# A third pair of weight chunks by seven products, and a search laid out by a table

## The chip, the cores and the metric

The kernel runs on one core of a Trainium2 chip. The metric is the time of one execution on the device, in microseconds (us). Three runs of the kernel before took 2345.66, 2346.05 and 2346.59 us; the median is 2346.05 us.

TensorE (PE in the profile) multiplies. VectorE (DVE), ScalarE (ACT) and GpSimd (POOL) do elementwise work, and SyncE (SP) issues nearly all transfers. Each engine runs its own instructions in order; they wait for each other through semaphores. Results of TensorE land in eight PSUM banks of 128 x 512 float32.

## The reference

Over 2048 tokens of width 1024 it computes a gated layer whose smaller half is set to zero, and a layer with a routed part, and adds both to the input:

```python
xn = (x - mean) / sqrt(var + 1e-5)
s = silu(xn @ w_gate.T)                       # 2752 units
s[the 1376 smallest |s| of each token] = 0
a = (s * (xn @ w_up.T)) @ w_down.T
h = relu(xn @ up_w) ** 2                      # 2048 units
shared = h @ down_w
routed = ((xn @ fc1_w) @ expert_w * (sum of the two largest of xn @ gate_w)) @ fc2_w
out = x + a + layernorm(shared + routed) * gamma + beta
```

## The kernel before

**Precision.** Each float32 operand is split into a high part, as TensorE rounds it, and a low part, the rest. A product is three matmuls: high by high, high by low, low by high (lines L880 to L882). All weights are split once, in block 0, and stored back to memory as pairs; later blocks load the pairs.

**Tiling.** There are four blocks of 512 tokens, that is four token tiles of 128. Weights come in chunks of 512 columns. The six gate chunks are gate 0 to 5 (gate 5, the "tail", has 392 columns here: 192 gate units, 8 routing logits, 192 up units), the five other up chunks up 0 to 4, and so on. One row of 128 weights of one chunk is a **granule**: one slot of a ring, and for the four token tiles 4 x 3 = 12 matmuls. A chunk has 8 granules. Granules have numbers m within a block, and all engines loop over the same m. The class Plan lays down at which m an engine reads which result. "At m" says only where an instruction stands in its engine's row: what it really waits for are semaphores.

**Seven products.** In blocks 1 to 3, gate 0 and 1 form a pair, and gate 2 and 3 another. A pair is a 2 x 2 block matrix product, done by seven block products instead of eight (Strassen's scheme in Winograd's form). Each has 4 granules of two token tiles, so of 6 matmuls. Four of the seven take mixed weights (T1 to T4, sums of weight rows), which VectorE makes in block 0 in `mix` (L1091 to L1096, once per four granules of a pair, two buffers `mixes`), and SyncE stores to `mixed_w` (L542). The results are put together by VectorE adds in `read_fast` (L1113, L1114). In block 0 the pairs are computed the plain way, 16 granules of 12 matmuls each.

**Order in a block.** Block 0: pair 0, pair 1 (32 granules), gate 5, gate 4, latent, hidden 0 and 1, routed 0 and 1, shared 0 and 1, hidden 2 and 3, up 4, shared 2, shared 3, up 0 to 3, out 0, out 1. Blocks 1 to 3 begin with gate 5 and then take both pairs by seven products. In block 0 a granule's weights are loaded raw, ScalarE makes the high part (L717), GpSimd the low part (L679); during the search GpSimd makes both (L675, L679).

**The search.** The threshold of each token is found bit by bit: 31 steps. In a step VectorE counts, in one pass each over 128 x 2816 magnitudes, for token tiles 0 and 1 (L1204), ScalarE for tiles 2 and 3 (L729), and VectorE settles the bit (L1193, L1196). The steps stand three granules apart in every engine's row, and between them stand VectorE's reads of other results. After the last step VectorE counts ties (L1212 to L1222) and masks: `mask` (L1266) multiplies the up values by "magnitude at least the threshold", group by group (a group is what one gate chunk holds), in the order gate 4, 5, 0, 1, 2, 3. GpSimd multiplies in the gate magnitudes (L702), TensorE turns the product chunks (L900, the first turn after granule out0 - 5, where out0 is the first granule of out 0), and out 0 can use them.

**Banks.** A chunk has four banks, one per token tile: set 0 is banks 0 to 3, set 1 banks 4 to 7, and chunks alternate. A chunk can't open before its banks were emptied by whoever reads the chunk before it in the same set. The first turn needs bank 0, which up 2 fills.

Of the kernel before, what the change touches and what calls it, by code (L numbers as in the profile page):

```python
# [60 lines left out]
FAST = 2  # L61
PRODUCTS = ["A11 B11", "S2 T2", "A12 B21", "S1 T1", "S4 B22", "S3 T3", "A22 T4"]
PRODUCT_BANK = [[4, 6, 0, 2, 4, 6, 0], [2, 4, 6, 4, 6, 0, 2]]
# [11 lines left out]
SET = {("gate", c): c % 2 for c in range(2 * FAST)}  # L75
SET.update({name: s % 2 for s, (name, n) in enumerate(_gates + _rest)})

# [4 lines left out]
def _first_pair(p):  # L82

    found = []
    for n in range(4 * HALF):
        c, k = 2 * p + n % 4 // 2, n // 4 + n % 2 * HALF
        found.append(Granule(("pair", p), n, ("gate", c), range(TILES), k == 0, n // 4 == HALF - 1 and n % 2 == 1,
                             (("gate", c), k)))
    return found


def _fast_pair(p):

    found = []
    for q, product in enumerate(PRODUCTS):
        right = product.split()[1]
        for k in range(HALF):
            if right[0] == "T":
                source = ("mixed", p, k, int(right[1]) - 1)
            else:  # L100
                source = (("gate", 2 * p + int(right[2]) - 1), k + HALF * (int(right[1]) - 1))
# [8 lines left out]

class Plan:


    def __init__(self, later):
        self.later = later
        found = []
        if later:
            found += _plain(*_gates[0])
        for p in range(FAST):
            found += _fast_pair(p) if later else _first_pair(p)  # L120
        for step in _gates[later:] + _rest:
            found += _plain(*step)
        self.granules = found
# [9 lines left out]
        self.read_at = {end[key] + LAG: key for key in end if key[0] in ("gate", "latent", "routed", "shared")}  # L133
        if later:
            del self.read_at[end[_gates[0][0]] + LAG]
            self.read_at[end[_gates[0][0]] + FAST_LAG] = _gates[0][0]
        self.read_up_at = {end[("up", g)] + (2 if g in (0, GROUPS[-1]) else LAG): ("up", g) for g in range(GC - 1)}
        self.search_at = {end[_gates[1][0]] + LAG + 1 + 3 * k: k for k in range(BITS)}

        order = [d for c in range(0, 2 * FAST, 2) for d in ((c + 1, c) if later else (c, c + 1))]  # L140
        order = [GC - 1, *order] if later else [*order, GC - 1]
        self.signs_before = {c: i + (i > order.index(GC - 1)) for i, c in enumerate([*order, GC - 2])}
# [1267 lines left out]
```

## Time and profile before

| | |
|---|---|
| median of three runs | 2346.05 us |
| profiled execution, its own time | 2345.21 us |
| its span | 2343.4 us |
| TensorE | 2330.9 us busy, 10576 matmuls |
| VectorE | 1602.3 us |
| ScalarE | 1054.3 us |
| GpSimd | 710.4 us |
| granted TensorE clock | 1.00 |

An engine's busy time is a sum over its instructions; the span is from the first to the last instruction of the core. TensorE is busy nearly without a break, so only two things change the time: how many matmuls there are, and whether TensorE has to wait.

### The profile page before, as it was taken

Reading aid. Unit: us, or ns where it says so; the run is one execution under the profiler, and the core shown is the slowest. Engines: PE = TensorE matmul, PEld = TensorE weight load, DVE = VectorE, ACT = ScalarE, POOL = GpSimd, SP = SyncE. Lnnn points to the kernel's source line nnn. Section 1 sums busy time; section 2 is a strip of 40 time slices with the busy share of each in tenths; the row PEclk is TensorE's granted clock in tenths of the full one; section 3 lists DMA queues with packets and bytes.
Section 4 is the critical chain, followed back from the end, with each engine's and each line's share of the span. In section 5 each row is a group of like instructions: output and inputs, shape, how many; then the busy total and the mean of one; then the engine's idle time right before and its main releaser. Section 6 shows DMA issues by size and latency. Waiting matters only on the chain.

```text
span 2343.4 us, 27578 instructions
## 1 busy us (share of the span) xinstructions
PE 2330.9 (99%) x10576; PEld 1940.5 (83%) x10576; DVE 1602.3 (68%) x1797; ACT 1054.3 (45%) x1199; POOL 710.4 (30%) x598
## 2 busy tenths in 40 slices
PE   8999999999999999999999999999999999999999
PEld 6888888888888888888888888888888888888887
DVE  4349999976255999876235699986723478997650
ACT  3248776133244877602124586740213368773010
POOL 5467878796450101040034010104004301000500
PEclk9999999999999999999999999999999999999999
DMA  7798889879886665655777666665667765556555
GB/s 284 283 391 293 292 271 324 292 241 316 279 294 199 193 195 192 214 191 187 235 247 245 208 193 194 194 210 189 206 218 259 251 192 195 194 193 213 183 189 180
DMA packets 182020, 545.83 MB, mean 233 GB/s; under 512 B 19328, under 2 KB 28544, under 8 KB 181888
## 3 DMA queue, kind: packets, MB, share of 16 engines
q1 hardware_dynamic: 181888, 544.06, 69.2%
q8 instruction: 84, 1.38, 0.2%
q14 instruction: 48, 0.39, 0.1%
HBM read 419.14 MB, written 124.85 MB: 232 GB/s over the span
## 4 chain that ended last, share of the span: by engine, by line
PE 99%; DMA 0%; DVE 0%; POOL 0%; DVEq 0%; ACT 0%; issue 0%
PE bank L880 32%; PE bank L882 32%; PE bank L881 32%; PE bank L900 2%; PE bank L891 1%; PE bank L973 0%; PE bank L974 0%; DMA rows<-x_dram 0%; DVEq L1035 0%; POOL expert L650 0%; DVE stats L1034 0%; POOL fc L654 0%; DVE acc L1275 0%; ACT expert L815 0%; DVE mv L1036 0%
## 5 line engine op out<-in xcount | busy, mean ns | idle before, releaser
L1204 DVE TENSOR_SCALAR_CACHE_REDUCE junk_v<-mag,cand 128x2816 bf16<-128x2816 f32 x248 | 780.3, 3146 | 8.8
L729 ACT ACTIVATE junk_s<-mag,cand 128x2816 uint8<-128x2816 f32 x248 | 655.6, 2644 | 222.6 <-DVE cand L1196 202.1
L880 PE MATMUL bank<-w,tok 128*128 128x512 f32 (+1 forms) x1108 | 426.3, 385 | 0.0
L882 PE MATMUL bank<-w,tok 128*128 128x512 f32 (+1 forms) x1108 | 424.9, 384 | 0.0
L881 PE MATMUL bank<-w,tok 128*128 128x512 f32 (+1 forms) x1108 | 424.8, 383 | 0.0
L679 POOL TENSOR_TENSOR w<-raw,w 128x512 fp32r<-128x512 f32 (+1 forms) x196 | 268.6, 1374 | 77.3 <-ACT w L717 67.6
L880 PE MATMUL bank<-w,prod_t 128*128 128x512 f32 x672 | 269.4, 401 | 0.0
L691 POOL TENSOR_TENSOR squares<-squares 128x512 f32<-128x512 f32 x64 | 69.0, 1078 | 640.4 <-ACT hidden L809 640.3
L882 PE MATMUL bank<-w,prod_t 128*128 128x512 f32 x672 | 262.8, 391 | 0.0
L881 PE MATMUL bank<-w,prod_t 128*128 128x512 f32 x672 | 261.9, 390 | 0.0
L880 PE MATMUL bank<-tok,w 128*128 128x512 f32 x640 | 249.0, 389 | 0.0
L881 PE MATMUL bank<-tok,w 128*128 128x512 f32 x640 | 249.0, 389 | 0.0
L882 PE MATMUL bank<-tok,w 128*128 128x512 f32 x640 | 249.0, 389 | 0.0
L882 PEld LDWEIGHTS bank<-w,tok 128*128 128x128 f32 x1108 | 208.0, 188 | 38.6
L881 PEld LDWEIGHTS bank<-w,tok 128*128 128x128 f32 x1108 | 208.1, 188 | 37.7
L880 PEld LDWEIGHTS bank<-w,tok 128*128 128x128 f32 x1108 | 208.0, 188 | 37.7
L869 ACT ACTIVATE prod_t<-bank 128x512 fp32r<-128x512 f32 x88 | 52.4, 596 | 402.2 <-PE bank L900 402.2
L702 POOL TENSOR_TENSOR prod<-prod,mag 128x512 f32<-128x512 f32 x88 | 122.2, 1411 | 338.4 <-DVE prod L1266 338.0
L880 PE MATMUL bank<-w,hidden 128*128 128x512 f32 x512 | 199.3, 389 | 0.0
L881 PE MATMUL bank<-w,hidden 128*128 128x512 f32 x512 | 199.2, 389 | 0.0
L882 PE MATMUL bank<-w,hidden 128*128 128x512 f32 x512 | 199.2, 389 | 0.0
L882 PEld LDWEIGHTS bank<-w,prod_t 128*128 128x128 f32 x672 | 126.1, 188 | 27.5
(140 smaller groups left out, 3307.4 us busy)
## 6 DMA issues: line engine op xcount, KB each, us to landing
w<-split_w SPq DMA_DIRECT2D x546, 512.0 KB, 4.2
split_w<-w SPq DMA_DIRECT2D x196, 512.0 KB, 4.9
w_more<-split_w SPq DMA_DIRECT2D x42, 512.0 KB, 4.9
w<-mixed_w SPq DMA_DIRECT2D x78, 256.0 KB, 3.2
rows<-x_dram SPq DMA_DIRECT2D x32, 512.0 KB, 5.2
raw<-w_down_dram SPq DMA_DIRECT2D x44, 256.0 KB, 4.0
raw<-w_up_dram SPq DMA_DIRECT2D x40, 256.0 KB, 3.5
w<-split_w SPq DMA_DIRECT2D x24, 392.0 KB, 3.7
```

Source lines behind the costliest of these rows:

```text
L679: pool.tensor_tensor(lo, words, hi, ALU.subtract).then_inc(lo_ready, 1)
L691: pool.tensor_tensor(squares[:, n, :], squares[:, n, :], squares[:, n, :], ALU.mult).then_inc(squared, 1)
L702: pool.tensor_tensor(prod[:, c, :, units], prod[:, c, :, units], mag[:, c, :, units], ALU.mult).then_inc(prod_ready, 1)
L729: act.activation(junk_s[:, :, :], mag[:, :, t, :], ACT.Sign, scale=-1.0, bias=cand[:, t:t + 1], accum_out=cnt[:, t:t + 1]).then_inc(counte ...
L869: act.activation(prod_t[0][:, c, :], banks[bank][:, :], ACT.Copy).then_inc(operand_hi, 1)
L880: pe.matmul(out, left[0], right[0], start=first, stop=False)
L881: pe.matmul(out, left[0], right[1], start=False, stop=False)
L882: return pe.matmul(out, left[1], right[0], start=False, stop=last)
L891: last = pe.transpose(banks[2 * (t % 2) + h][:, k * P:(k + 1) * P], rows_of(t)[:, (h * HK // 2 + k) * P:(h * HK // 2 + k + 1) * P], ident[ ...
L900: last = pe.transpose(banks[bank][:, t * P:(t + 1) * P], prod[:, c, t, :], ident[:, :])
L1204: dve.tensor_scalar(junk_v[:, :, :], mag[:, :, t, :], cand[:, t:t + 1], float(1 - (GATED - KEPT)), ALU.is_lt, ALU.add, accum_out=cnt[:, t: ...
```

## The change

A third pair is formed of gate 4 and up 4 (`PAIRS`). Block 0 computes it the plain way, after pair 1 and ahead of gate 5, and mixes its weights; blocks 1 to 3 take it by seven products, straight after pair 1. Up 4 leaves its place between hidden 3 and shared 2. As its results are sums now, VectorE applies the signs to up 4 in one instruction, `sign_up`.

The search begins after the last gate chunk: in block 0 after gate 5, with the first step at m = 60 instead of 52, and in blocks 1 to 3 after the third pair, with the first step at m = 96 instead of 76. Its layout is now written as tables (`VECTOR_TILES`, `STEP_AT`), which hold what stood there before: two tiles on each engine, three granules apart. Shared 2 and shared 3 are interleaved by half chunks, so that both close within 4 granules, at the end of 16. The squares of hidden 2 and 3 stand one granule apart instead of two; in blocks 1 to 3 their low parts, and those of hidden 0 and 1, are made by GpSimd instead of VectorE. The buffer of latent's high part moves into `acc`, and ScalarE waits for what that needs.

```diff
+PAIRS = [(("gate", 0), ("gate", 1)), (("gate", 2), ("gate", 3)), (("gate", GC - 2), ("up", GC - 2))]
+FAST = len(PAIRS)
-PRODUCT_BANK = [[4, 6, 0, 2, 4, 6, 0], [2, 4, 6, 4, 6, 0, 2]]
+PRODUCT_BANK = [[4, 6, 0, 2, 4, 6, 0], [2, 4, 6, 4, 6, 0, 2], [4, 6, 0, 4, 6, 0, 2]]
-_gates = [(("gate", GC - 1), HK), (("gate", GC - 2), HK)]
+_tail = (("gate", GC - 1), HK)
-          (("hidden", 2), HK), (("hidden", 3), HK), (("up", GC - 2), HK), (("shared", 2), HK), (("shared", 3), HK)]
+          (("hidden", 2), HK), (("hidden", 3), HK), (("shared", 2), HK), (("shared", 3), HK)]
+VECTOR_TILES = [range(2) for k in range(BITS)]
+STEP_AT = [3 * k for k in range(BITS + 1)]
...
+        at = [m for m, g in enumerate(found) if g.step in (("shared", 2), ("shared", 3))]
+        found[at[0]:at[-1] + 1] = [found[m] for m in sorted(at, key=lambda m: (found[m].k // HALF, m))]
...
-        self.search_at = {end[_gates[1][0]] + LAG + 1 + 3 * k: k for k in range(BITS)}
+            last = end["fast", FAST - 1, len(PRODUCTS) - 1]
+            self.fast_at.update({last + 2: (FAST - 1, 5), last + 3: (FAST - 1, 6)})
+            self.signs_at[last + 4] = (FAST - 1, 6)
+            first = last + 5
+        else:
+            first = end[_tail[0]] + LAG + 1
+        self.search_at = {first + STEP_AT[k]: k for k in range(BITS)}
...
-        self.hidden_at = {end[("hidden", i)] + LAG + 1 + 2 * t: (i, t) for i in range(SC) for t in range(TILES)}
+        self.hidden_at = {end[("hidden", i)] + LAG + 1 + (2 if i < 2 else 1) * t: (i, t) for i in range(SC) for t in range(TILES)}
...
+                        if b:
+                            pool.wait_ge(squared, b * SC * TILES + i * TILES + t + 1)
+                            pool.tensor_tensor(hidden[1][:, n, :], squares[:, n, :], hidden[0][:, n, :],
+                                               ALU.subtract).then_inc(hidden_lo, 1)
...
+            def sign_up(b):
+                ks = slice(4 * (GC - 2), 4 * (GC - 1))
+                dve.wait_ge(signs_done, b * (GC + 1) + PLANS[b].signs_before[GC - 2] + 1)
...
+                dve.scalar_tensor_tensor(out=prod[:, ks, :, :], in0=positive[:, ks, :, :], scalar=-1.0,
+                                         in1=prod[:, ks, :, :], op0=ALU.add, op1=ALU.mult).then_inc(up_signed, 1)
```

VectorE's row in block 0, just ahead of the first pass of the search. `positive` and `mag` of 128x2048 are the reading of a whole gate chunk, the small operations onto `prod` the end of reading gate 5, `junk_v` the count. Before:

```order
L1160 SCALAR_TENSOR_TENSOR prod<-positive,bank 128x128
L1160 SCALAR_TENSOR_TENSOR prod<-positive,bank 128x64
L1132 TENSOR_SCALAR positive<-mag 128x2048
L1136 TENSOR_SCALAR mag<-mag 128x2048
L1345 MEMSET cand 128x4
L1204 TENSOR_SCALAR junk_v,cnt<-mag,cand 128x2816 x2
```

And now (line numbers are those of the changed kernel):

```order
L1199 SCALAR_TENSOR_TENSOR prod<-positive,bank 128x128
L1199 SCALAR_TENSOR_TENSOR prod<-positive,bank 128x64
L1389 MEMSET cand 128x4
L1243 TENSOR_SCALAR junk_v,cnt<-mag,cand 128x2816 x2
L1232 TENSOR_SCALAR refused<-cnt 128x4
L1235 SCALAR_TENSOR_TENSOR cand<-cand,refused 128x4
```

The reading of gate 4 is gone from this place; the search starts straight after gate 5 has been read.

VectorE's row in block 0, after the count of ties: masks, and between them the reads of up 1 and up 2 (`prod<-positive,bank`). Before:

```order
L1266 SCALAR_TENSOR_TENSOR prod<-mag,thr,prod 128x4x128 x4
L1266 SCALAR_TENSOR_TENSOR prod<-mag,thr,prod 128x2x128 x4
L1266 SCALAR_TENSOR_TENSOR prod<-mag,thr,prod 128x4x128 x4
L1181 SCALAR_TENSOR_TENSOR prod<-positive,bank 128x4x128 x4
L1266 SCALAR_TENSOR_TENSOR prod<-mag,thr,prod 128x4x128 x4
L1181 SCALAR_TENSOR_TENSOR prod<-positive,bank 128x4x128 x4
L1266 SCALAR_TENSOR_TENSOR prod<-mag,thr,prod 128x4x128 x4
L1378 TENSOR_TENSOR prod_t_54<-bank,prod_t_53 128x512 x3
```

And now:

```order
L1308 SCALAR_TENSOR_TENSOR prod<-mag,thr,prod 128x4x128 x4
L1220 SCALAR_TENSOR_TENSOR prod<-positive,bank 128x4x128 x4
L1308 SCALAR_TENSOR_TENSOR prod<-mag,thr,prod 128x2x128 x4
L1308 SCALAR_TENSOR_TENSOR prod<-mag,thr,prod 128x4x128 x8
L1220 SCALAR_TENSOR_TENSOR prod<-positive,bank 128x4x128 x4
L1308 SCALAR_TENSOR_TENSOR prod<-mag,thr,prod 128x4x128 x4
L1422 TENSOR_TENSOR prod_t_54<-bank,prod_t_53 128x512 x3
```

The read of up 1 moves ahead of the masks of groups 5 and 0. What stands ahead of the read of up 2 is the same set of instructions as before. The read of up 0, which stood right behind the last step of the search, now stands two steps ahead of its end, in all blocks.

## Rows read from the trace of the kernel before

**Rows 1.** The page: the chain that ended last, share of the span by engine

```profile
PE 99%; DMA 0%; DVE 0%; POOL 0%; DVEq 0%; ACT 0%; issue 0%
```

**Rows 2.** Waits of PE: us in total, times, longest

```profile
PE bank L891 <- DVE rows L1050: 8.8, 2, 7.9
```

**Rows 3.** Timeline of PE (start, length, instruction): first matmuls of stretches

```profile
37.74 0.39 PE L880 MATMUL bank<-w,tok 128*128 128x512 f32 x1
124.78 0.34 PE L880 MATMUL bank<-w,tok 128*128 128x392 f32 x1
141.80 0.39 PE L880 MATMUL bank<-w,tok 128*128 128x512 f32 x1
```

**Rows 4.** Windows: the search of block 0, then of block 1

```profile
168.00:428.00 260.00, 260.00 (x1148) 215.06 (x1147) 253.85 (x229) 191.63 (x168) 205.39 (x209) 1.00 0.87 297
741.00:999.00 258.00, 258.00 (x1140) 213.71 (x1139) 235.46 (x229) 192.63 (x168) 17.26 (x16) 1.00 0.62 198
```

**Rows 5.** Timeline of DVE: mixes start; below, landing of the mixes' stores

```profile
82.84 0.69 DVE L1091 TENSOR_TENSOR mixes<-raw 128x512 f32<-128x512 f32 x1 [9.25 <-DMA mixed_w<-mixes]
96.10 1.00 DVE L1091 TENSOR_TENSOR mixes<-raw_more 128x512 f32<-128x512 f32 x1 [3.78 <-DMA mixed_w<-mixes]
120.26 0.92 DVE L1091 TENSOR_TENSOR mixes<-raw_more 128x512 f32<-128x512 f32 x1 [8.75 <-DMA mixed_w<-mixes]
...
DMA to landing us min/median/max: 6.2/6.7/8.1
```

**Rows 6.** Timeline of POOL: low parts of granules 14, 30 and 38

```profile
66.52 1.29 POOL L679 TENSOR_TENSOR w<-raw_more,w 128x512 fp32r<-128x512 f32 x1 [3.69 <-ACT w L717]
...
116.32 1.29 POOL L679 TENSOR_TENSOR w<-raw_more,w 128x512 fp32r<-128x512 f32 x1 [2.59 <-ACT w L717]
...
135.74 1.04 POOL L679 TENSOR_TENSOR w<-raw,w 128x392 fp32r<-128x392 f32 x1 [2.59 <-ACT w L717]
```

**Rows 7.** Timeline, block 0: gate 5 read, first pass of the search

```profile
145.68 0.26 ACT L786 ACTIVATE mag<-bank 128x128 f32<-128x128 f32 x1
...
151.23 1.33 DVE L1160 SCALAR_TENSOR_TENSOR prod<-positive,bank 128x128 f32<-128x128 uint8 x8
...
168.13 3.15 DVE L1204 TENSOR_SCALAR_CACHE_REDUCE junk_v<-mag,cand 128x2816 bf16<-128x2816 f32 x1
```

**Rows 8.** Timeline, block 0: up 4 read, last settling, masks, up 2 read, first turn

```profile
368.07 2.47 DVE L1181 SCALAR_TENSOR_TENSOR prod<-positive,bank 128x512 f32<-128x512 uint8 x4
...
428.00 0.58 DVE L1193 TENSOR_SCALAR refused<-cnt 128x4 int32<-128x4 f32 x1
...
447.62 13.57 DVE L1266 SCALAR_TENSOR_TENSOR prod<-mag,thr,prod 128x512 f32<-128x512 f32 x12 [4.77 <-issue]
...
468.79 2.47 DVE L1181 SCALAR_TENSOR_TENSOR prod<-positive,bank 128x512 f32<-128x512 uint8 x4
...
479.31 0.60 PE L900 MATMUL bank<-ident,prod 128*128 128x128 f32 x4
```

**Rows 9.** Timeline, block 1: two steps, up 0, masks, up 1 and 2, first turn

```profile
978.05 3.15 DVE L1204 TENSOR_SCALAR_CACHE_REDUCE junk_v<-mag,cand 128x2816 bf16<-128x2816 f32 x1
...
984.91 3.15 DVE L1204 TENSOR_SCALAR_CACHE_REDUCE junk_v<-mag,cand 128x2816 bf16<-128x2816 f32 x1
...
996.77 2.73 DVE L1181 SCALAR_TENSOR_TENSOR prod<-positive,bank 128x512 f32<-128x512 uint8 x4 [5.53 <-PE bank L882]
...
1017.13 13.12 DVE L1266 SCALAR_TENSOR_TENSOR prod<-mag,thr,prod 128x512 f32<-128x512 f32 x12 [3.73 <-issue]
...
1032.57 4.90 DVE L1266 SCALAR_TENSOR_TENSOR prod<-mag,thr,prod 128x512 f32<-128x512 f32 x4
...
1042.94 2.73 DVE L1266 SCALAR_TENSOR_TENSOR prod<-mag,thr,prod 128x512 f32<-128x512 f32 x4
...
1053.02 0.60 PE L900 MATMUL bank<-ident,prod 128*128 128x128 f32 x4
```

**Rows 10.** Windows: the first 13 us

```profile
0.00:13.00 13.00, 3.91 (x16) 3.14 (x16) 5.24 (x13) 5.04 (x9) 3.45 (x8) 1.00 0.84 317
```

More of the change, by code:

```diff
@@ L85, in _first_pair @@
     for n in range(4 * HALF):
-        c, k = 2 * p + n % 4 // 2, n // 4 + n % 2 * HALF
-        found.append(Granule(("pair", p), n, ("gate", c), range(TILES), k == 0, n // 4 == HALF - 1 and n % 2 == 1,
-                             (("gate", c), k)))
+        name, k = PAIRS[p][n % 4 // 2], n // 4 + n % 2 * HALF
+        found.append(Granule(("pair", p), n, name, range(TILES), k == 0, n // 4 == HALF - 1 and n % 2 == 1, (name, k)))
     return found
@@ L159, in __init__ @@
         self.tokens_load += [out1 + 7, out1 + 11]
-        if later:
-            self.fast_at = {end[("fast", p, q)] + FAST_LAG: (p, q) for p in range(FAST) for q in range(len(PRODUCTS))}
-            self.signs_at = {end[("fast", p, q)] + FAST_LAG + 3: (p, q) for p in range(FAST) for q in (5, 6)}
 TURN_AFTER = [5, 9, 13, 17]
@@ L254, in highs @@
     return 2 * TILES + b * HIGHS + HIGH_FROM[kind] + n
-NV = TILES // 2
-NS = TILES - NV
-VECTOR_TILES, SCALAR_TILES = range(NV), range(NV, TILES)
+SCALAR_TILES = [range(len(tiles), TILES) for tiles in VECTOR_TILES]
 SQUARE_LAG = 2
@@ L852, in _ @@
                         square_hidden(b, *plan.hidden_at[m])
-                    for n, t in enumerate(SCALAR_TILES):
-                        if m - n in plan.search_at:
-                            count(b, plan.search_at[m - n], n, t)
+                    for n in range(TILES - 1):
+                        k = plan.search_at.get(m - n)
+                        if k is not None and n < len(SCALAR_TILES[k]):
+                            count(b, k, n, SCALAR_TILES[k][n])
                     for t in range(TILES):
@@ L1098, in read_fast @@
             def read_fast(b, p, q):
-                c, d = 2 * p, 2 * p + 1
+                c, d = (name[1] for name in PAIRS[p])
+                right = mag if PAIRS[p][1][0] == "gate" else prod
                 for j in range(2):
@@ L1136, in read_gate @@
                     dve.tensor_scalar(bits, bits, 0x7FFFFFFF, None, ALU.bitwise_and).then_inc(mag_ready, 1)
+            def sign_up(b):
+                ks = slice(4 * (GC - 2), 4 * (GC - 1))
+                dve.wait_ge(signs_done, b * (GC + 1) + PLANS[b].signs_before[GC - 2] + 1)
+                for j in range(2):
+                    for q in (4, 5):
+                        bank, value = emptied(b, ("fast", FAST - 1, q, j))
+                        dve.wait_ge(bank_emptied[bank], value)
+                dve.scalar_tensor_tensor(out=prod[:, ks, :, :], in0=positive[:, ks, :, :], scalar=-1.0,
+                                         in1=prod[:, ks, :, :], op0=ALU.add, op1=ALU.mult).then_inc(up_signed, 1)
             def read_logits(b):
@@ L1261, in mask @@
                 for t in range(TILES):
-                    bank, value = emptied(b, ("up", g, t) if g < GC - 1 else ("gate", g, t))
-                    dve.wait_ge(bank_emptied[bank], value)
+                    if b and g == GC - 2:
+                        dve.wait_ge(up_signed, b)
+                    else:
+                        bank, value = emptied(b, ("up", g, t) if g < GC - 1 else ("gate", g, t))
+                        dve.wait_ge(bank_emptied[bank], value)
                     if g == GC - 1:
```

75 lines of the change are left out of this document (42 added, 33 removed).

## The prediction

> **What bounds the kernel now.** I read the chain that ended last first: TensorE holds 99% of it [rows 1]. The list of TensorE's waits shows why: its largest entry is 8.8 us, at the start; nothing later is worth a row [rows 2]. So the time is the sum of TensorE's instructions, and the timeline gives their pace. In block 0, 32 granules lie between 37.74 and 124.78 [rows 3]: 2.72 us a granule, 226.7 ns a matmul of 512 columns. The 8 granules of gate 5 take 17.02 us, 2.13 each. Less work for TensorE is time won, as long as nobody makes it wait, so next I read how close the others are. The windows show VectorE busy for 253.85 of 260 us in the search of block 0, and 235.5 of 258 in block 1 [rows 4]. GpSimd, which in block 0 splits weights, is busy 205 us in the first and 17 in the second. Two places matter: block 0, where VectorE has nothing to spare, and the first turn, where its work must be done.
>
> **The gain.** Gate 4 and up 4 cost 2 x 8 x 12 = 192 matmuls in a block. By seven products they cost 7 x 4 x 6 = 168. That is 24 fewer, in three blocks 72; 72 x 226.7 ns = 16.3 us. Block 0 has as many as before. If nothing waited, the profiled execution would take 2345.2 - 16.3 = 2328.9 us.
>
> **Block 0, the preparation of weights.** Low parts have to be ready before TensorE takes a granule. That of granule 14 is ready at 66.52 + 1.29 = 67.8 and TensorE takes it at 37.74 + 14 x 2.72 = 75.8, 8.0 us later. For granule 30 the same reckoning gives 117.6 against 119.3, for granule 38 136.8 against 137.5 [rows 3, 6]. So 16 pair granules cost TensorE 43.5 us and the preparation 49.8, and the lead is eaten to 0.8 us. The reason is in the mixes: each waits for the landing of a store [rows 5], SyncE sends the next raw loads only when a mix is made, and three rounds take 120.26 - 82.84 = 37.4 us, 12.5 for four granules. The third pair adds four such rounds, and I see nothing that would speed them up. The low part of granule 54, the former 38, is then due at 136.8 + 49.8 = 186.6, and TensorE could take it at 37.74 + 48 x 2.72 + 6 x 2.13 = 181.1. TensorE waits 5.5 us in all here. It doesn't add to what follows, since VectorE is later still.
>
> **Block 0, the search.** Before, it began at 168.13, 4 us after gate 4. Now it begins after gate 5. ScalarE reads gate 5 at 145.68, after its own splits, and VectorE is done with it at 152.6 [rows 7]. With 49.8 us on top, the first pass starts at 202.5, 34.3 us later than before. TensorE's work ahead of out 0 is the same as before, so the turns should still come at 479.3. From the first pass to the last settling VectorE worked without a break for 259.9 us [rows 7, 8]. The same 31 steps, 16 low parts and reads stand there now, except the read of up 4 (2.4 us), now ahead of the search. The last settling is due at 428.0 + 34.3 - 2.4 = 459.9. Before, the read of up 2 began 40.8 us after the settling [rows 8], and the same instructions lie between, in another order. So bank 0 is free for the first turn at 459.9 + 40.8 + 0.7 = 501.4, against 479.3: 22.1 us late. The nearer stops on the way (up 3 needs the read of up 1, at 482.9 to 485.3 against 468.2; shared 2 needs the low parts of hidden 3) are inside this.
>
> This takes every mask at its slow rate. Twelve masks took 13.57 us beside GpSimd's work, four without it took 2.73 [rows 8, 9]. While TensorE stands still, GpSimd has no slot to fill until the first mask is made; so I give the first four the fast rate, 2.4 us less: 19.7 us late. If all masks had it, it would be 12.7. The ends are 12.7 and 22.1, the value 19.7.
>
> On this term the Trainium skill has a rule: SBUF — State Buffer, Who interferes with whom, says that a VectorE instruction with two SBUF inputs and a GpSimd instruction that reads SBUF exclude each other for a whole instruction. By it the masks would cost their own 0.7 us plus at most one GpSimd instruction each, and the term would lie between the same two ends; the rows agree so far. The count passes, with one such input, would be untouched.
>
> **Blocks 1 to 3.** Here TensorE reaches the end of up 0 a fixed 20 granules before the first turn, in both kernels. In block 1 the read of up 0 ended at 999.5 and the turn came at 1053.0: 53.5 us [rows 9]. Behind that read there stand now two more steps (2 x 6.86 = 13.7), then settling, ties and the pause before the masks (1017.13 - 999.5 = 17.6), masks of four groups with the read of up 1 (1037.5 - 1017.1 = 20.3), and the first tile of up 2, 0.7: 52.3 us. So 1.2 us remain of 15. The read of up 0 itself should be on time: 29 steps (199 us), four reads of 2.7 and about 6 us before the first pass make 216, TensorE takes 88 x 2.72 = 239. VectorE also gets rid of the low parts of the squares; GpSimd, at 17 of 258 us, takes them for nothing. `sign_up` is one instruction for four reads, inside those 6 us. I put this term at 0, with 0 to 2 us a block as its bounds.
>
> **The sum.** 2345.2 - 16.3 + 19.7 = 2348.6 us for an execution like the profiled one, which lay 0.8 under the median: 2349.4. Both terms are large and nearly cancel.
>
> **The rivals.**
> First, block 0 keeps up and the gain comes through. For it: the rounds of mixes are a chain of latencies, not a full memory, so an earlier raw load would shorten them. Against it: VectorE is without idle time afterwards. If preparation kept TensorE's pace (6.3 us less) and gate 5 were read as it closes (145.7 - 141.8 = 3.9 less), the delay would be 9.5: 2339.2 us. With no delay at all it would be 2329.7. I give both 17%.
> Second, the slower one: blocks 1 to 3 each wait at the first turn. The place is bank 0, held by up 2; it decides once VectorE is more than 1.2 us late behind up 0, and each further microsecond counts three times. For it: the squares of hidden 2 and 3 stand closer, so ScalarE's counts can come later, and GpSimd's products slow the masks. Against it: VectorE was idle 22.5 of 258 us in block 1's search, and with the read of up 1 among them the masks meet fewer products. At 3 us late: 3 x 1.8 = 5.4 more, 2354.8 us. 25%.
> Third, TensorE's clock falls in the waits of block 0. In the first 13 us TensorE was busy 3.9 us and the granted clock read 1.00 [rows 10], so the waits so far left it at the upper level, 2.4 GHz. A granule at 1.2 GHz would cost 5.4 instead of 2.7 us; two of them lost make 5.4 us and 2354.8. 3%.
> The Trainium skill (TensorE: Matmul & The Clock Gate, Why this matters for your kernels) warns that idle gaps between matmuls drop the clock to half; by it the waits of block 0 would add some microseconds. The first window doesn't bear it out.
>
> **How the numbers follow.** The forecast, 55%: 2349.4, by its bounds 2342.4 to 2351.8. About 0.2%, 4.7 us, is what a measurement of this kernel can tell from no change: 2341.4 to 2350.7 count as the same. Of the forecast's 55 I put 46 there and 9 above; the first rival gives 17 to faster; of the second and third, 24 to slower and 4 to the same. Faster 0.17, same 0.50, slower 0.33. The range must reach into the second rival and to the edge of the first: 2342 to 2355.
>
> **What would show it.** TensorE has 10576 - 72 = 10504 matmuls. In block 0 its waits appear at low parts of weights around 160 to 187 us (some 5.5 us) and at VectorE's results until the first turn, which comes near 499 instead of 479.3; the first pass starts near 202.5, the last settling near 460. Out 0 and out 1 of block 0 keep their length. A block 1 to 3 is 5.4 us shorter, with its first turn on time. The forecast is wrong if the first pass starts before 195, if VectorE's 257 us between first pass and last settling shrink, or if blocks 1 to 3 show waits before their first turn.

## The result, and the profile after

The changed kernel is slower: 2356.11 us (median of five runs, 2355.81 to 2361.0) against 2346.05 in the same comparison, a ratio of 1.0047 with a 95% interval of 1.0032 to 1.0062. The forecast was 2349.4, its range 2342 to 2355. The profiled execution took 2355.98 us, its span is 2354.2: 10.8 us more than before, where 3.4 more were forecast.

The list of TensorE's waits (us in total, times, longest), where [rows 2] had one entry worth a line:

```profile
PE bank L919 <- DVE rows L1078: 8.7, 2, 7.8
PE bank L928 <- DVE prod L1220: 7.1, 1, 7.1
PE bank L908 <- DVE hidden L1383: 6.6, 2, 3.5
PE bank L908 <- POOL w L697: 3.1, 4, 0.9
PE bank L908 <- ACT mag L809: 1.6, 2, 1.0
```

The first is the start, as before. The others are all in block 0: the first turn waits for the read of up 2 (L1220), shared 2 for low parts of hidden, three granules of the third pair and one of gate 5 for low parts of weights (L697), and the openings of up 4 and gate 5 for banks that ScalarE has yet to read (L809). The chain that ended last, by engine, which was all TensorE in [rows 1], says the same:

```profile
PE 79%; DVE 13%; DMA 4%; issue 1%; SPq 1%; ACT 1%; POOL 1%; DVEq 0%; ACTq 0%
```

The later blocks did what was forecast. TensorE's first matmuls of block 1 and block 2, before and after:

```profile
622.34 0.34 PE L880 MATMUL bank<-w,tok 128*128 128x392 f32 x1
...
1196.03 0.34 PE L880 MATMUL bank<-w,tok 128*128 128x392 f32 x1
```

```profile
649.08 0.34 PE L908 MATMUL bank<-w,tok 128*128 128x392 f32 x1
...
1217.51 0.34 PE L908 MATMUL bank<-w,tok 128*128 128x392 f32 x1
```

A block takes 568.4 us instead of 573.7, 5.3 less, three times. But block 1 begins 26.7 us later. 26.7 - 3 x 5.3 = 10.8, the whole difference. So everything is in block 0, whose stops answer to [rows 7, 8] (VectorE, then TensorE's first turn and the matmuls behind it):

```profile
202.97 3.15 DVE L1243 TENSOR_SCALAR_CACHE_REDUCE junk_v<-mag,cand 128x2816 bf16<-128x2816 f32 x1
...
461.98 0.17 DVE L1232 TENSOR_SCALAR refused<-cnt 128x4 int32<-128x4 f32 x1
...
481.80 3.18 DVE L1308 SCALAR_TENSOR_TENSOR prod<-mag,thr,prod 128x512 f32<-128x512 f32 x4 [4.12 <-issue]
...
484.89 2.47 DVE L1220 SCALAR_TENSOR_TENSOR prod<-positive,bank 128x512 f32<-128x512 uint8 x4
487.29 16.01 DVE L1308 SCALAR_TENSOR_TENSOR prod<-mag,thr,prod 128x256 f32<-128x256 f32 x12
...
503.22 2.47 DVE L1220 SCALAR_TENSOR_TENSOR prod<-positive,bank 128x512 f32<-128x512 uint8 x4
```

```profile
503.95 1.11 PE L928 MATMUL bank<-ident,prod 128*128 128x128 f32 x4 [7.09 <-DVE prod L1220]
504.72 0.78 PE L908 MATMUL bank<-w,tok 128*128 128x512 f32 x1
505.29 0.63 PE L909 MATMUL bank<-w,tok 128*128 128x512 f32 x1
505.72 0.63 PE L910 MATMUL bank<-w,tok 128*128 128x512 f32 x1
...
510.64 0.39 PE L909 MATMUL bank<-w,tok 128*128 128x512 f32 x1
510.87 0.39 PE L910 MATMUL bank<-w,tok 128*128 128x512 f32 x1
```

The first pass starts at 202.97 us (202.5 forecast), the first turn at 503.95 (499 forecast, 479.31 before). Behind the turn, matmuls start 0.43 us apart instead of 0.23: 512 columns in 0.43 us are the lower level of the clock, 1.2 GHz, and it lasts about 4 us. The windows show it too (the third number from the right is the granted clock, as a share of the upper level):

```profile
366.00:382.00 16.00, 12.53 (x50) 9.99 (x49) 15.79 (x14) 11.43 (x12) 13.37 (x13) 0.89 0.86 286
395.00:412.00 17.00, 13.87 (x55) 10.98 (x54) 16.79 (x15) 10.95 (x8) 13.19 (x13) 0.90 0.90 322
492.00:505.00 13.00, 5.91 (x27) 4.75 (x26) 13.00 (x12) 0.00 (x0) 9.92 (x7) 0.87 0.53 182
505.00:518.00 13.00, 13.00 (x58) 10.55 (x57) 6.32 (x11) 4.53 (x9) 5.76 (x6) 0.87 0.29 87
```

### The profile page after: what moved, and what is told of

It is laid out like the page before. It is cut to its first block, busy times and chain, and to the rows that moved or that the text cites. A ratio compares the mean times of both kernels' runs of the same rounds, so it can differ in the third digit from the quotient of the medians.

```text
span 2354.2 us, 27758 instructions
## 1 busy us (share of the span) xinstructions
PE 2323.3 (99%) x10504; PEld 1930.9 (82%) x10504; DVE 1632.0 (69%) x1810; ACT 1090.9 (46%) x1261; POOL 819.7 (35%) x674
## 4 chain that ended last, share of the span: by engine, by line
PE 79%; DVE 13%; DMA 4%; issue 1%; SPq 1%; ACT 1%; POOL 1%; DVEq 0%; ACTq 0%
PE bank L908 25%; PE bank L910 25%; PE bank L909 25%; DVE junk_v L1243 8%; DMA mixed_w<-mixes 2%; PE bank L928 2%; DMA split_w<-w 1%; DVE prod L1308 1%; DVE refused L1232 1%; SPq L555 1%; SPq L551 1%; DVE cand L1235 1%; DVE junk_v L1251 1%; PE bank L919 1%; DVE hidden L1383 0%
## 5 line engine op out<-in xcount | busy, mean ns | idle before, releaser
L908 PE MATMUL bank<-w,tok 128*128 128x512 f32 (+1 forms) x952 | 367.0, 386 | 4.7 <-POOL w L697 3.1
L909 PE MATMUL bank<-w,tok 128*128 128x512 f32 (+1 forms) x952 | 364.9, 383 | 0.0
L910 PE MATMUL bank<-w,tok 128*128 128x512 f32 (+1 forms) x952 | 364.8, 383 | 0.0
L697 POOL TENSOR_TENSOR w<-raw,w 128x512 fp32r<-128x512 f32 (+1 forms) x188 | 254.7, 1359 | 94.3 <-ACT w L739 85.3
L908 PEld LDWEIGHTS bank<-w,tok 128*128 128x128 f32 x952 | 179.2, 188 | 39.2 <-POOL w L697 4.7
L910 PEld LDWEIGHTS bank<-w,tok 128*128 128x128 f32 x952 | 179.1, 188 | 32.4
L909 PEld LDWEIGHTS bank<-w,tok 128*128 128x128 f32 x952 | 179.2, 188 | 31.7
L700 POOL TENSOR_TENSOR w<-w 128x512 fp32r<-128x512 f32 x78 | 116.3, 1515 | 135.8 <-ACT w L868 135.7
```

Of the source, the lines that this page charges most:

```text
L697: pool.tensor_tensor(lo, words, hi, ALU.subtract).then_inc(lo_ready, 1)
L700: pool.tensor_tensor(slot_of(g)[:, 1, :], slot_of(g)[:, 1, :].bitcast(F32), slot_of(g)[:, 0, :], ALU.subtract).then_inc(pool_lo, 1)
L908: pe.matmul(out, left[0], right[0], start=first, stop=False)
L909: pe.matmul(out, left[0], right[1], start=False, stop=False)
L910: return pe.matmul(out, left[1], right[0], start=False, stop=last)
```

## The experiments

The kernel before ran beside every group of them, at 2345.95 to 2346.47 us. "The first pass", "the ties" and "out 0" are their starts in block 0; in the changed kernel they stand at 202.97, 463.45 and 518.86 us.

**e1: the third pair's mixes left out**

```diff
-MIXES = FAST * HALF
+MIXES = 2 * HALF
-                    n = p * HALF + k
+                    n = (p * HALF + k) % MIXES
```

> The changed kernel with the four sets of mixes of the third pair not made in block 0; wherever they are loaded later, the mixes of the first pairs are loaded in their place, so gate chunk 4 and up chunk 4 come out with other values. Theory (block 0 loses time in three pieces: preparing the third pair, a longer first search pass, and the later reads and masks behind them): without the last quarter of the preparation the granules from 33 on start at the normal step of 2.8 to 3.3 us, the first search pass begins at about 197 us instead of 203, everything behind it is some 5 to 6 us earlier, and the run takes about 2350 us. Rival A (the delay is set by VectorE's chain of searches and masks alone, and the rounds of preparation beside it cost nothing of their own): the pass still begins within 2 us of 203, and the time stays at 2355 to 2356. Rival B (the low clock in block 0 is the loss): the shares of clock stay near 0.9 in the stretches 366:412 and 492:518 and the time stays at 2355.

2345.09 us, 11.0 under the changed kernel: twice what the theory gave, and both rivals are out. The first pass starts at 193.15 and out 0 at 509.50, 9.8 and 9.4 us earlier: the start of the search passes on to the end of block 0 nearly one to one. The granted clock is still low in places (0.93 in 395:412, 0.70 in 492:505), so it isn't what made the difference. The profiled execution of e1 took 2346.56 us, 9.4 less than that of the changed kernel. A surprise stands in the window where the third pair would be mixed; first the changed kernel, then e1 (the last two numbers are DMA share and GB/s):

```profile
137.00:162.00 25.00, 23.36 (x102) 18.72 (x101) 11.84 (x13) 4.76 (x8) 10.89 (x8) 1.00 0.82 294
```

```profile
137.00:162.00 25.00, 25.00 (x112) 20.69 (x111) 0.28 (x1) 7.26 (x13) 16.10 (x13) 1.00 1.03 405
```

With mixes the queues carry 294 GB/s, without them 405. So the rounds of mixes are not slow because memory is full.

**e2: low parts of the squares on GpSimd in block 0 too**

```diff
-                        if b:
+                        if True:
...
-                    if b == 0 and m - SQUARE_LAG - 1 in plan.hidden_at:
+                    if False and m - SQUARE_LAG - 1 in plan.hidden_at:
```

> The changed kernel with one condition altered: in block 0 too GpSimd, not VectorE, makes the low parts of the squares of hidden, as both already do in blocks 1 to 3. Theory: VectorE's chain in block 0 (first pass to the last mask) is what makes bank 0 late, and it is rid of some 16 us of work: bank 0 is free about 14 to 16 us earlier than at 503.9 us, near 489, and the time is 2340 to 2343 us. Rival A (GpSimd's queue then delays the low parts of the weights, since it works some 205 of 260 us there already and gets about 20 us more): TensorE waits in L697's name instead, and the time is 2350 to 2356. Rival B (clock): the wait moves and the low clock stays, 2352 or more.

2352.12 us, 4.0 under the changed kernel, where 13 to 16 were expected. The first pass starts 0.9 later, the ties come 5.2 earlier. Two groups of VectorE in the search, first of the changed kernel, then of e2 (count | busy, mean ns of one | idle before):

```profile
L1232 DVE TENSOR_SCALAR refused<-cnt 128x4 int32<-128x4 f32 x30 | 14.0, 468 | 2.5 <-ACT junk_s L751 1.0
L1235 DVE SCALAR_TENSOR_TENSOR cand<-cand,refused 128x4 int32<-128x4 int32 x30 | 12.8, 426 | 1.0
```

```profile
L1232 DVE TENSOR_SCALAR refused<-cnt 128x4 int32<-128x4 f32 x31 | 18.2, 586 | 4.8 <-ACT junk_s L751 2.3
L1235 DVE SCALAR_TENSOR_TENSOR cand<-cand,refused 128x4 int32<-128x4 int32 x30 | 16.4, 548 | 1.0
```

Each settling is two instructions on 4 numbers, 0.16 us each when nothing is in the way; they take up to 1.27 us beside GpSimd. All 62 take 28.2 us in the changed kernel and 35.9 here. So nearly 8 of the 18.4 us saved go to these, and 2.3 to longer waits for ScalarE. Another 2.0 us of the 5.2 are lost between the ties and the first turn. The time lies in the ranges of both rivals, and TensorE's waits for low parts of weights grew as A said, to 8.7 us in eight. But they don't set the time: the first turn still waits 6.6 us for the read of up 2. Nor does the clock, which is low behind that wait as it was.

**e3: one count of VectorE cut short in the last four steps of block 0**

```diff
-                    dve.tensor_scalar(junk_v[:, :, :], mag[:, :, t, :], cand[:, t:t + 1], float(1 - (GATED - KEPT)),
+                    ks = slice(0, 1 if b == 0 and i == 1 and k >= BITS - 4 else GK)
+                    dve.tensor_scalar(junk_v[:, ks, :], mag[:, ks, t, :], cand[:, t:t + 1], float(1 - (GATED - KEPT)),
```

> The changed kernel in which, in block 0 alone, VectorE's second count of the last four search steps covers 1 of the 22 chunks (the threshold of the second tile is so chosen by a wrong count in those steps). This takes about 12 us from VectorE's chain of searches and nothing from anything else. Theory (the end of the chain sets the start of block 1 one to one): the first pass of ties begins 10 to 12 us earlier than at 463.5 us, up 1, up 2 and the first turn come as much earlier, and the time is 2344 to 2346 us. Rival A (the chain waits at each step for ScalarE's count or for the reads of shared 2, so that less work on VectorE is only a longer wait): less than 4 us is gained, 2352 or more. Rival B (clock: the low share is a loss beside the chain): about 2 us more or less than the chain gives.

2351.13 us, 5.0 less, between the theory and rival A: the ties come 5.9 us earlier for 11.2 us less work. The rows of one step (VectorE) show who takes over:

```profile
444.78 3.15 DVE L1244 TENSOR_SCALAR_CACHE_REDUCE junk_v<-mag,cand 128x2816 bf16<-128x2816 f32 x1
447.85 0.08 DVE L1244 DVE_READ_ACCUMULATOR junk_v<-mag,cand 128x1 f32 x1
447.97 0.35 DVE L1244 TENSOR_SCALAR_CACHE_REDUCE junk_v<-mag,cand 128x128 bf16<-128x128 f32 x1
448.24 0.09 DVE L1244 DVE_READ_ACCUMULATOR junk_v<-mag,cand 128x1 f32 x1
450.38 0.95 DVE L1232 TENSOR_SCALAR refused<-cnt 128x4 int32<-128x4 f32 x1 [2.05 <-ACT junk_s L751]
```

ScalarE's own two counts take 5.6 us, VectorE's two 6.4. A step can't fall below the first, so in a step without a read only 0.86 us can be won, in one with a read up to 2.8. The claim "the end of the chain sets the start of block 1" holds (5.9 us at the ties, 5.6 at out 0); "work taken off VectorE is time won" doesn't.

**e4: gate 5 between the second and the third pair in block 0**

```diff
+            if p == 2 and not later:
+                found += _plain(*_tail)
...
-            first = end[_tail[0]] + LAG + 1
+            self.read_at[end[_tail[0]] + 1] = _tail[0]
+            first = end[PAIRS[2][0]] + LAG + 1
```

> The changed kernel in which block 0 makes gate chunk 5, which belongs to no pair, between the second and the third pair and not behind the third. Its read then no longer stands between the third pair and the first search pass, and the preparation of the third pair's weights gets a granule step of 24 us of head start. Theory: the first pass begins 10 to 13 us earlier, near 191 us, and since the chain behind it sets the start of block 1, the time is 2343 to 2346 us. Rival A (the preparation, not the read of gate 5, ends the wait of the first pass): the third pair ends where it ended, and the gain is 5 us or less, 2351 or more. Rival B (the later stages of the search meet reads of shared and hidden at other steps and lose what the start gained): 2350 to 2356 with the first pass early and the ties pass at 460 or later.

2356.35 us: nothing won, and times and rows are near those of rival B. The first pass comes at 198.69 (of which 1.3 is an earlier start of granule 0), the ties at 460.33, out 0 at 517.81. Two long waits of TensorE stand in its list that the changed kernel hasn't:

```profile
PE bank L915 <- DVE prod L1227: 10.0, 1, 10.0
...
PE bank L915 <- DVE prod L1206: 6.5, 1, 6.5
```

The second is gate 5's read, stuck behind a mix of the third pair. That mix didn't wait for a store but for its raw weights:

```profile
150.08 0.69 DVE L1126 TENSOR_TENSOR mixes<-raw 128x512 f32<-128x512 f32 x1 [16.17 <-DMA raw<-w_up_dram]
```

The first is the read of up 1: as the search now ends earlier in VectorE's row, twelve masks stand ahead of that read instead of four, and up 3 can't open.

**e5: four buffers for the mixes instead of two**

e1 pointed at the rounds of mixes, and VectorE's waits name what ends them, a store. These are the waits in 37:175 in the changed kernel:

```profile
DVE mixes L1119 <- DMA mixed_w<-mixes: 85.1, 10, 14.5
```

```diff
+MIX_SETS = 4
...
-        mixes = [over(f"mixes{i}", [P, 4, N], F32, u_at + 4 * i * N * 4) for i in range(2)]
+        mixes = [over(f"mixes{i}", [P, 4, N], F32, u_at + 4 * i * N * 4) for i in range(MIX_SETS)]
...
-                if n >= 2:
-                    dve.wait_ge(mixes_stored[n % 2], 16 * (n // 2))
+                if n >= MIX_SETS:
+                    dve.wait_ge(mixes_stored[n % MIX_SETS], 16 * (n // MIX_SETS))
```

> The changed kernel with four buffers for the mixes instead of two (the added two lie where nothing else lives in block 0 until hidden 0); nothing else is altered and nothing is left out. In the trace of the changed kernel VectorE waits 85 us in ten rounds for the store of the mixes made two rounds earlier, and the DMA share is 0.82 there, while without the third pair's mixes (run e1) it reached 1.03 and 405 GB/s in 137:162. Theory: a round is a chain of latencies (store, mix, next raw loads), not a full memory; with the wait for the store gone the preparation keeps TensorE's pace of 2.72 us a granule, TensorE's waits for low parts in 160:187 vanish, the first pass begins near 194 us instead of 203, and the time is 2345 to 2348 us. Rival A (memory: 3.5 MB for four granules can't come faster beside the rest): the share of DMA rises to 1.0 in 87:137 and the rounds shrink by less than 1 us; first pass near 199, 2351 to 2353. Rival B (the raw loads wait for the mixes, 52.8 us on SyncE's queue, and that loop closes without the stores too): rounds stay 12.3 to 12.5 us and the time 2355 to 2356.

2343.88 us, 12.2 under the changed kernel and no slower than e1 (2345.09), which leaves the mixes out. The same waits now:

```profile
DVE positive L1161 <- ACT mag L810: 23.7, 5, 12.8
DVE mixes L1120 <- DMA raw<-w_gate_dram: 12.7, 2, 6.4
DVE mixes L1120 <- DMA raw_more<-w_gate_dram: 10.6, 2, 7.5
```

The stores are gone from the list; what is left are raw loads that keep pace. TensorE takes the 16 granules of the third pair in 43.5 us, its own rate, and waits for no low part. The first pass starts at 191.67 (194 expected). Rival A's memory limit isn't there: it wanted a share of 1.0 in 87:137, which reads 0.73 and 0.81, and in 62:87, where it reads 1.03, TensorE is busy without a break. This also falsifies a sentence of the prediction, that nothing in sight would speed up the rounds; its first rival, which called them a chain of latencies, came nearer.

**e6 and e7: four buffers with gate 5 between the pairs, and with GpSimd's low parts**

Edits: e5 and e4 together, with gate 5's read ahead of the mixes at the same granule; e7 adds e2's. (Where the expectation of e6 has a mix of e4 wait for a store, the row above shows a raw load.)

> Run e5's four buffers together with run e4's place of gate chunk 5 (between the second and the third pair in block 0), its read put ahead of the mixes that stand at the same granule. Run e4 alone won nothing; its trace has waits of TensorE at the granules 35, 41 and 42, for low parts and for the read of gate 5, which stood behind a mix that waited for a store. Theory: with those waits gone both edits count; the third pair ends near 181 us, the first pass begins near 187, and since all behind it hangs on that start, the time is 2338 to 2341 us. Rival A (the start of the search can't be turned into an earlier end, since ScalarE's two counts and the reads of shared and hidden set the later steps): first pass near 187 but the ties pass later than 452, 2345 to 2348. Rival B (the third pair, now behind gate 5, is late all the same, for its raw loads): first pass at 195 or later, 2347 to 2352.

> Run e6 with run e2's edit on top: GpSimd, not VectorE, makes the low parts of the squares in block 0. Run e2 took the 19 us of low parts off VectorE but its 31 settlings grew from 28.2 to 35.9 us beside the busier GpSimd, and some steps waited, so the ties pass came only 6.1 us sooner after the first pass. Theory: the same here, 3 to 4 us under e6, 2334 to 2338 us, with the first turn of block 0 no longer waiting for up 2. Rival (in e6 the chain is already near TensorE's pace, so the edit only moves waits to the low parts of weights on GpSimd): equal to e6 or up to 3 us above it.

2346.03 and 2344.31 us: neither is below e5 (2343.88), and both theories missed. (e6 has the time of its rival A, but not its reason, ties behind 452; e7 is 1.7 us under e6, where 3 to 4 were expected.) In e6 the first pass comes at 187.80, as expected, 3.9 ahead of e5, the ties only 1.4 ahead, out 0 2.7 behind. The 10.0 us wait for the read of up 1 is there as in e4, behind twelve masks. An earlier start of the search is worth nothing when the masks that it brings forward stand before a read that TensorE needs.

**e8: shared 2 and 3 not interleaved**

```diff
-        at = [m for m, g in enumerate(found) if g.step in (("shared", 2), ("shared", 3))]
-        found[at[0]:at[-1] + 1] = [found[m] for m in sorted(at, key=lambda m: (found[m].k // HALF, m))]
```

> The changed kernel with one part of the change undone: shared 2 and shared 3 are not interleaved but stand one behind the other, in all blocks. In the changed kernel TensorE waits in block 0 some 10 us beyond its pace at the granules 121, 122, 130 and 131 of shared 2, for low parts of hidden 2 and 3. Theory: those waits lie inside the time that TensorE must give to VectorE anyway before the first turn; they go or move, and the time stays at 2355 to 2357 us. Rival (they are part of the loss): 2346 to 2349, and the first turn of block 0 is as much earlier.

2360.74 us, 4.6 above the changed kernel: neither came. The waits didn't vanish but grew, as the second half of shared 2 now asks for hidden 3 four granules sooner:

```profile
PE bank L906 <- DVE hidden L1381: 14.7, 2, 11.3
```

The interleaving is thus a part of the change that pays. From first pass to ties VectorE took 262.5 us instead of 260.5, and the first pass itself was 1.1 later behind granule 0; how the rest arises was not settled.

**e9: up 2 read ahead of the masks**

The rows of the changed kernel put twelve masks (487.29 to 503.22) between the reads of up 1 and up 2, and bank 0 waits for the second.

```diff
         self.mask_at[out0 + 3] = GROUPS[-1]
+        if not later:
+            self.mask_at = dict(zip([out0 - 14, out0 - 5, out0 - 4, out0 - 1, out0 + 2, out0 + 4], GROUPS))
```

> The changed kernel with the masks of block 0 in other places of VectorE's row: only the four masks of gate chunk 4 stay ahead of the reads of up 1 and up 2; those of chunks 5, 0, 1 and 2, which stood between the two reads, come behind the read of up 2, among the turns. Nothing is left out. In the changed kernel the read of up 1 ends at 487.3 us, twelve masks follow (15.9 us), and only then is up 2 read, whose bank 0 the first turn needs (503.9); TensorE waits 7.1 us there, and the granule behind it runs at a clock of 0.87. Theory: bank 0 is free at about 488, TensorE, which ends granule 163 near 496, waits for nothing there, the low clock goes too, and the time falls by 7.1 plus some 2 us: 2346 to 2348. Rival A (the masks moved back make the products and so the later turns late): the wait comes back as waits between the turns or at the first granules of out 0, 2352 to 2356. Rival B (only the clock or only the wait goes): 2349 to 2350 where the low clock stays.

2356.58 us (2352.85 to 2357.11): no gain, though the wait of 7.1 us and the slow matmuls behind it are gone. Against its own granule 0, out 0 is 7.3 us earlier than in the changed kernel, block 1 only 2.9. What came between is rival A: TensorE waits 2.8 us for the low part of turn 4, at granule 171. And granule 0 itself began at 42.47 us in this profile instead of 38.51. The rows show where that arose: in VectorE's scaling of the third token tile.

```profile
20.31 5.66 DVE L1080 TENSOR_SCALAR rows<-rows,mv,rstd 128x1024 f32<-128x1024 f32 x1
```

In the changed kernel the same instruction begins at 20.37 us and takes 1.92, and it takes 1.9 in all thirteen other profiles, that of the kernel before included. GpSimd makes five low parts in a row meanwhile, here from 19.15 to 25.43 us. TensorE then waits 2.6 us more for the scaled rows, and the matmuls behind that stand 0.43 us apart for a moment. The edit touches nothing so early, and e13 below, which contains it, began at 38.22. So the late start isn't its work, but hides what it gains: the profile is 1.0 us longer than the changed kernel's. The fastest run, 2352.85, is 3.3 us under the changed kernel, near the 2.9 that the rows give; whether the other runs had the late start, and what makes it come, no run here shows.

**e10 and e11: four buffers with the early read, and with GpSimd's low parts**

Edits: e5 and e9 together; e11 adds e2's.

> Run e5 (four buffers for the mixes) with run e9's order of reads and masks; nothing is left out. In e5 the read of up 1 ends at 475.2, up 2 is read at 491.1 to 493.5, and TensorE waits 7.1 us for it at a clock that falls to 0.89. Theory (two independent losses of block 0, one before the search and one behind it): the gains add, 12 from the buffers and 9 from the order: 2334 to 2337 us, faster than the kernel before by some 10 us. Rival A (TensorE comes to the turn so early that the turned chunks or the low parts of the later groups are late): 2338 to 2342. Rival B (as in e9, the moved masks only move the wait): 2343 to 2345.

> Run e10 with run e2's edit on top (GpSimd makes the low parts of the squares in block 0 too); nothing is left out. Run e2 gained 4 us over the changed kernel and e7 under 2 over e6, all by an earlier end of the search. Theory: in e10 the turn no longer waits for the search by way of up 2, only up 3's first granule by way of up 1, and TensorE's wait of 2.8 us at granule 130 of shared 2 goes; so 1 to 3 us under e10. Rival (the busier GpSimd lets TensorE wait for low parts of weights, as the 8.7 us in eight waits of run e2): as e10 or 1 to 2 us above it.

2339.16 and 2337.11 us, ratios to before of 0.9970 (0.9960 to 0.9981) and 0.9965 (0.9951 to 0.9978): faster than the kernel before. e11 is 2.0 us under e10, as its theory had it. e10 is 2 us short of its own theory and in the range of rival A, and its rows show the place. TensorE, then VectorE:

```profile
510.16 0.60 PE L931 MATMUL bank<-ident,prod 128*128 128x128 f32 x4
513.52 0.47 PE L911 MATMUL bank<-w,prod_t 128*128 128x512 f32 x1 [2.77 <-DVE prod_t L1425]
...
514.56 0.63 PE L911 MATMUL bank<-w,prod_t 128*128 128x512 f32 x1
```

```profile
499.22 13.55 DVE L1311 SCALAR_TENSOR_TENSOR prod<-mag,thr,prod 128x512 f32<-128x512 f32 x8
512.70 1.41 DVE L1425 TENSOR_TENSOR prod_t<-bank,prod_t 128x512 fp32r<-128x512 f32 x2
```

Eight masks in a row, 1.7 us each beside GpSimd, stand before turn 4's low part. The wait is 2.8 us, and the slow matmuls behind it cost another 1.5.

**e12 and e13: the last four masks five granules later**

```diff
-            self.mask_at = dict(zip([out0 - 14, out0 - 5, out0 - 4, out0 - 1, out0 + 2, out0 + 4], GROUPS))
+            self.mask_at = dict(zip([out0 - 14, out0 - 5, out0 - 4, out0 - 1, out0 + 2, out0 + 9], GROUPS))
```

in e11 (that is e12) and in e9 (e13).

> Run e11 (four buffers for the mixes, up 2 read ahead of the masks, low parts on GpSimd) with the last four masks of block 0 five granules further back; nothing is left out. In e11 VectorE makes eight masks in a row at 1.7 us beside GpSimd before it gives turn 4's chunk its low part; TensorE waits 2.7 us for it at granule 171 and the next one runs slow, 6.10 and 4.63 us for 3.2 each. Theory: with four masks between instead of eight the wait and the slow granule go, 4.3 us: 2332 to 2334 us. Rival (the masks, moved back, hold up the products and norms of out 0, so that the wait comes back further on): 2336 to 2338.

> Run e9 with the last four masks five granules further back, without the four buffers and with the low parts on VectorE as in the changed kernel; nothing is left out. Run e9 took 7.1 us of waiting away before the first turn, and its time didn't fall. Theory: 4.4 us of it came back at the granules 171 and 172, as in e10 and e11, and the rest is its start: granule 0 began at 42.47 us in its profile, at 38.51 in the changed kernel's. Then this run is 7 to 9 us under the changed kernel, 2347 to 2349, with granule 0 near 38 us in most runs. Rival (the start is late whenever the order of block 0 is this one, or TensorE has to give the time back elsewhere): 2352 or more.

2332.74 us (2332.35 to 2333.16) and 2347.57: both theories hit. e12 is faster than the kernel before, ratio 0.9942 (0.9928 to 0.9956), and 23.4 us under the changed kernel. Block 1 begins at 625.62 us, 3.3 later than before the change, where it was 26.7. TensorE's waits in it, and the first stretch of the turns (granted clock 1.00):

```profile
PE bank L922 <- DVE rows L1081: 8.7, 2, 7.7
PE bank L911 <- POOL w L700: 2.3, 2, 1.3
PE bank L911 <- POOL fc L675: 0.4, 1, 0.4
```

```profile
492.00:505.00 13.00, 13.00 (x67) 10.76 (x66) 11.55 (x13) 5.68 (x9) 13.00 (x10) 1.00 0.77 261
```

e13 has none of the buffers and is 8.5 us under the changed kernel, with granule 0 at 38.22. Against granule 0 its block 1 begins 8.3 us earlier than in the changed kernel. The three edits nearly add: 12.2 (buffers, e5) + 8.5 (reads and masks, e13) + 2.0 (low parts, e11 over e10) = 22.7, measured 23.4.

## Why the prediction was wrong, step by step

**Right.** The matmuls are 10504. A block 1 to 3 is 5.3 us shorter (5.4), its first turn on time; the second rival, three waits there, didn't come. The first pass, 202.97 against 202.5, was right too, and so was the delay of TensorE by the preparation: latent began 6.4 us behind its pace, 5.5 forecast, though the waits were spread from granule 34 on, not only at the end, and 1.6 us of them were for ScalarE's reads, which the prediction didn't have. That prediction and rows agree there doesn't make its reason complete: it saw nothing that would speed up the rounds of mixes, and with two more buffers the first pass came 11.3 us earlier (e5). The sentence "it doesn't add to what follows" was misleading as well: the preparation set the start of the search, and that start passes through to block 1, as e1 and e5 show.

**The step that failed** is the term for block 0's delay: 19.7 us, measured 26.7. In its pieces:

- *Up to the first pass*: 0.5 later than forecast. Granule 0 began 0.8 later than before.
- *First pass to last settling*: 257.4 forecast, 259.0 measured, 1.6 more. The prediction took the read of up 4 out of the search (2.4 us) and kept all else. But durations there aren't fixed: the 16 low parts of squares took 18.4 us instead of 16.5. In e8, where only the interleaving is undone, they took 16.0; how they fall against GpSimd's work is a likely reason, but wasn't shown.
- *Last settling to the first turn*: 39.1 forecast, 42.0 measured, 2.9 more. This is the step that failed most: the prediction gave the first four masks the fast rate, for 2.4 us less in all. They had it nearly (3.1 us), but the twelve behind them took 15.9 us, dearer than any group before the change (13.5 for twelve, 5.3 for four). All sixteen took 19.0 us, about what they had taken before (18.8), and not 16.4. So 2.6 of the 2.9 us are the masks. From the last settling to the ties it took 0.7 us more, since the settling's second half met GpSimd (1.23 us, before 0.16), and from there to the masks 0.4 less. The turn came 24.6 us late, beyond the upper bound of 22.1.
- *The first turn to out 0*: 2.1 us more than before (14.9 against 12.8, as out 0 began at 492.14 before), for the clock. This is the third rival, which got 3%. Its mechanism is real; its price, 5.4 us, was too high.

0.5 + 1.6 + 2.9 + 2.1 is 7.1; that is the difference between 26.7 and 19.7 to a rounding. With 0.4 from the later blocks it gives the 7.4 us by which the span missed.

The 2.4 us were also reckoned with the wrong row. Twelve masks in 13.57 us [rows 8] are 4.5 for four, and against 2.73 that is 1.8 us less, not 2.4; the 2.4 fits only the last four, at 5.3. The lower end of the term, 12.7 with all masks fast, took that dearest rate for all sixteen: 18.8 - 4 x 2.73 is 7.9 us less than 22.1, so 14.2.

**The clock was misread.** [rows 10] gave 1.00 for the first 13 us (the next 13 read 1.00 too), and the prediction took from it that waits leave the clock alone. The timeline of the kernel before, right behind that window, says otherwise:

```profile
13.11 0.80 PE L880 MATMUL bank<-fc,expert 128*128 128x512 f32 x1 [0.39 <-POOL fc L654]
13.70 0.63 PE L881 MATMUL bank<-fc,expert 128*128 128x512 f32 x1
14.13 0.63 PE L882 MATMUL bank<-fc,expert 128*128 128x512 f32 x1
...
15.54 0.39 PE L880 MATMUL bank<-fc,expert 128*128 128x512 f32 x1
```

After the idle start the matmuls stand 0.43 us apart, and then fall to 0.23. The granted clock of these windows didn't show it, the spacing of matmuls did. The warning of the Trainium skill (TensorE: Matmul & The Clock Gate, Why this matters for your kernels) was right for this kernel, and was set aside on a row that couldn't carry it. Its price is small here: 2.1 us behind the first turn. The slow stretches at 375 and 406 us cost nothing, since TensorE waits 7.1 us at the turn afterwards.

**Why the range missed.** Its upper end, 2355, left no room for several small excesses in one direction. Two of the four pieces were stretches where VectorE works beside GpSimd, so they went wrong together. The same dependence shows in e2, where small settlings grew from 28.2 to 35.9 us. On the rule of the Trainium skill that the prediction weighed (SBUF — State Buffer, Who interferes with whom), the trace agrees for the masks (0.7 or 1.1 to 1.8 us) and for the counts, 3.146 us each in every kernel. Two things go beyond what the prediction took from it. Instructions with one tensor input that aren't counts were held up too, a settling's first half up to 1.27 us (e2). And the scaling in e9, 0.8 us where nothing held it, took 5.66 beside five GpSimd operations of 1.3 us in a row, so more than one of them can go by.

## What to carry to other kernels

When a stage is paced by rounds, look at what ends its wait before calling the pace given: here a wait for the landing of a store two rounds back, with the DMA share at 0.82, asked for another buffer, not for less work. When work moves ahead of a search or a sort whose end everything hangs on, count what stands in the row between that end and the first thing the busiest engine needs; only that has to stand there. And behind a long forecast wait of TensorE, add some matmuls at the low clock, read from their spacing elsewhere in the trace.

## What the runs showed of the hardware

- Behind the 7.1 us wait at the first turn the next matmuls of 512 columns started 0.43 us apart instead of 0.23, some eight of them in the changed kernel, five in e5. Behind the first wait for shared 2 (3.5 us) it was six in the changed kernel and none in e8. All nine waits of 6.5 us and more behind the start, in block 0 of these profiles had such matmuls behind them, five to fourteen; waits of 2.2 to 3.8 us had them or not. What decides wasn't settled.
- Two VectorE instructions on 128 x 4 numbers take 0.16 us each, and up to 1.3 beside GpSimd. The 62 of a search of 260 us took 25.7 us in e8, 28.2 in the changed kernel, 35.9 in e2 and 40.5 in e7. In the last two GpSimd makes the low parts of the squares as well; why e7 has more than e2 wasn't settled.
- The queues carried 404 GB/s over 25 us in e5 (62:87), at a share of 1.03, where the changed kernel moved 294 GB/s in the same window at 0.82.
- One VectorE instruction on 128 x 1024 numbers, 0.8 us where nothing held it, took 1.9 us beside GpSimd's five low parts in fourteen profiles and 5.66 us in one (e9), where the gate chunks of block 0 began some 4 us late.
